# The order of TensorE's work within an attention step: scores, all projection parts, transposes, products, then the tail tasks

## What is computed

```python
q = (x @ Wq).reshape(B, T, H, 2 * DH).transpose(0, 2, 1, 3)      # B=8, T=512, H=16, KV=4, DH=32
k, v = ...                                                        # 4 key/value heads, repeated 4 times
s1 = jnp.einsum('bhtd,bhsd->bhts', q1, k1) * scale + mask         # q1, q2, k1, k2 after rope
s2 = jnp.einsum('bhtd,bhsd->bhts', q2, k2) * scale + mask
diff = softmax(s1) - lam * softmax(s2)
out = jnp.einsum('bhts,bhsd->bhtd', diff, v)
out = group_norm(out, over=(T, 2 * DH)) * gn_w + gn_b
x = layernorm(x + out.reshape(B, T, 2 * H * DH) * (1 - LAMBDA_INIT) @ Wo)
w_e = top-2 weights of softmax(x @ gate_w.T)
x = layernorm(x + sum_e w_e * ((silu(x @ w_gate[e]) * (x @ w_up[e])) @ w_down[e]))
```

## Time and profile before

| | |
|---|---|
| median of 3 runs | 2086.36 us (2084.78 to 2091.78) |
| the profiled execution | 2085.87 us, its span 2084.0 us |
| busy over the span | PE 1708.1 (82%), DVE 1374.3 (66%), ACT 1170.9 (56%), POOL 581.3 (28%) |
| instructions | 37142 |

### The profile page before, as it was taken

The page is one execution under the profiler, slowest core; times in us unless marked ns, Lnnn a source line. Parts: engine busy times, 40 slices in busy tenths (PEclk is TensorE's granted clock), DMA queues, the critical chain, the costliest instruction groups (busy, mean ns, idle before and its releaser), DMA issues. The chain is left out here.

```text
span 2084.0 us, 37142 instructions
## 1 busy us (share of the span) xinstructions
PE 1708.1 (82%) x9698; PEld 1264.6 (61%) x9699; DVE 1374.3 (66%) x3225; ACT 1170.9 (56%) x3378; POOL 581.3 (28%) x496
## 2 busy tenths in 40 slices
PE   4578899899889989889889989873999999999500
PEld 3455556655655655655655655542999999999400
DVE  2578878878888888887887897734333333333366
ACT  2467778787787886877877787832222222222133
POOL 2132232322332232241242243011633332000265
PEclk7799999999999999999999999985999999999755
DMA  7965464565474574565556455213533342232288
GB/s 249 295 168 165 132 169 136 159 177 141 144 211 123 147 214 125 144 199 155 142 173 190 136 166 146 83 67 140 167 118 122 107 127 81 70 101 87 86 283 275
DMA packets 143494, 318.74 MB, mean 153 GB/s; under 512 B 16720, under 2 KB 19408, under 8 KB 141296
## 3 DMA queue, kind: packets, MB, share of 16 engines
q1 hardware_dynamic: 114576, 243.17, 41.1%
q0 software_dynamic: 13792, 46.54, 6.6%
q10 hardware_dynamic: 14976, 27.27, 3.4%
HBM read 215.21 MB, written 109.05 MB: 156 GB/s over the span
## 5 line engine op out<-in xcount | busy, mean ns | idle before, releaser
L803 ACT ACTIVATE expd<-S,neg_max 128x128 f32<-128x128 f32 (+3 forms) x1024 | 531.2, 537 | 167.0 <-DVE neg_max L958 165.1
L958 DVE TENSOR_REDUCE neg_max<-S 128x2 f32<-128x768 f32 (+3 forms) x384 | 399.1, 1039 | 209.9 <-PE S L647 205.4
L989 DVE SCALAR_TENSOR_TENSOR mixed<-expd,rho 128x384 f32<-128x384 f32 (+3 forms) x512 | 328.6, 662 | 0.1
L643 PE MATMUL S<-kT,qT 128*128 128x256 f32 (+2 forms) x1024 | 283.5, 380 | 40.4 <-DMA qT<-parts_rows 25.0
L658 PE MATMUL PTp<-ident,mixed 128*128 128x128 f32 x1280 | 216.9, 285 | 81.7 <-DVE mixed L989 79.4
L815 ACT ACTIVATE probsT<-PTp 128x512 f32<-128x512 f32 (+2 forms) x384 | 205.2, 534 | 122.8 <-PE PTp L658 117.8
L643 PEld LDWEIGHTS S<-kT,qT 128*128 128x128 f32 x1024 | 164.7, 196 | 139.2 <-issue 95.7
L1369 ACT ACTIVATE xT_hi<-xTp 128x512 fp32r<-128x512 f32 x72 | 43.2, 600 | 358.3 <-DVE yo L1545 352.7
L697 PE MATMUL tail<-wo,ctxT 128*128 128x512 f32 x480 | 229.3, 603 | 16.9 <-ACT ctxT L854 9.3
L535 POOL TENSOR_TENSOR swapped<-swapped,rope_t 128x512 f32<-128x512 f32 x80 | 103.3, 1291 | 493.9 <-DVE swapped L951 493.9
L803 ACT ACTIVATION_READ_ACCUMULATOR expd<-S,neg_max 128x1 f32 x1024 | 218.0, 213 | 0.0
(11 more groups left out here) (224 smaller groups left out, 3641.2 us busy)
## 6 DMA issues: line engine op xcount, KB each, us to landing
qT<-parts_rows SPq DMA_DIRECT2D x256, 256.0 KB, 4.5
parts_rows<-parts SPq DMA_DIRECT2D x160, 256.0 KB, 2.1
wqk<-wqk_split SPq DMA_DIRECT2D x75, 512.0 KB, 6.2
xin<-expert_in_rows SPq DMA_DIRECT2D x72, 256.0 KB, 3.0
expert_out_rows<-yo ACTq DMA_DIRECT2D x72, 256.0 KB, 3.2
kT<-parts_rows SPq DMA_DIRECT2D x64, 256.0 KB, 4.4
x<-in_x SPq DMA_DIRECT2D x8, 1024.0 KB, 7.2
x_rows<-x SPq DMA_DIRECT2D x8, 1024.0 KB, 7.2
```

The source lines that it names most:

```text
L643: nc.tensor.matmul(S[s % 2][:, k * slot:k * slot + w], qT[kv % 2][:, 2 * h + c, i * P:(i + 1) * P], kT[kv][:, c, 0:w], start=(k % per_bank ...
L803: ex = nc.scalar.activation(expd[s % 3][:, k * slot:k * slot + w], S[s % 2][:, k * slot:k * slot + w], ACT.Exp, bias=neg_max[s % 3][:, k:k ...
L958: nc.vector.tensor_reduce(neg_max[s % 3][:, 0:k], v, AX, ALU.max, negate=True).then_inc(max_ready, 1)
L989: ins = nc.vector.scalar_tensor_tensor(out=mixed[sl % 3][:, a * 256:a * 256 + w], in0=e2, scalar=rr[:, i, h:h + 1], in1=e1, op0=ALU.mult, ...
```

## The change

`body` of PE calls the same pieces in another order within the step. Before: scores, transposes, parts of groups already begun, tail tasks, parts of a group that begins here, values. After: scores, parts of groups already begun, parts of a group that begins here, transposes, values, tail tasks. All other engines' programs stay as they are.

```diff
                 for s, kv, u in steps(b, first, last):
                     scores(b, s, u, kv)
+                    for new in (False, True):
+                        for idx, c in parts_of(s, last, new):
+                            project(b, first, idx, c)
                     if lagged(b, s, LAG_T, first):
                         transposes(*lagged(b, s, LAG_T, first))
-                    for idx, c in parts_of(s, last, False):
-                        project(b, first, idx, c)
+                    if (s - LAG_V) % NU in LAST_OF and lagged(b, s, LAG_V, first):
+                        values(*lagged(b, s, LAG_V, first), tile_no(b, s, LAG_V))
                     if not first:
                         for task in TAIL_PE.get(s, []):
                             tail_task(b - 1, 1 - par, task)
-                    for idx, c in parts_of(s, last, True):
-                        project(b, first, idx, c)
-                    if (s - LAG_V) % NU in LAST_OF and lagged(b, s, LAG_V, first):
-                        values(*lagged(b, s, LAG_V, first), tile_no(b, s, LAG_V))
```

## The result

The changed kernel is slower: 2116.6 us (median of 4 runs, 2112.1 to 2117.6) against 2089.1 (4 runs of the kernel before beside them, 2084.8 to 2094.6), a ratio of 1.0126 with an interval of 1.0095 to 1.0157. The forecast was 2075 with 2106 as the upper end. The profiled execution took 2115.69 us.

What follows compares the result with a forecast made beforehand. TensorE leads (busy 146.28 of 163.08 us a batch), but VectorE and ScalarE are near full and set the pace in turn. Terms -9.1 +0.7 -1.8 -2.5 +3.9 -2.4 = -11.2 take 2085.9 to 2075; 8-in-10 range 2060 to 2106.

Steps and rivals of the forecast that it cites:

- Steps 45 to 5: Parts fill TensorE's waits for `mixed`; VectorE's max of step 5 starts 1.3 us earlier, carried on: -9.1 us in all.
- Rival 1: The gain is swallowed: VectorE or SP's DMA chain holds step 12 or the stretch behind it; 2084 us, chance 0.20.
- Step 12: ScalarE is the bound to step 17; two parts ahead of the transposes make its copy 0.1 late: +0.7 us in all.
- Steps 16 to 18: Products wait for `ctxT` about 1.1 us; a part fills step 18's wait; step 19 starts 0.25 earlier: -1.8 us in all.
- Steps 24 to 26: Four parts ahead of the transposes; the projection VectorE waits for ends 0.35 earlier, late exps have slack: -2.5 us in all.
- Steps 29 and 31: TensorE waits about 0.45 for `xl` in step 29, products meet `ctxT` 0.2 early in step 31: +3.9 us in all.
- Steps 34 to 43: ScalarE 1.2 late, TensorE waits 2.5 before step 37; early products give back in step 39: net -2.4 us in all.
- rival 3: TensorE's clock falls at step 37 in each of six batches: +12, which gives 2087 us, chance 0.08.
- rule about transposes: PE-mode transposes don't count as busy work for the clock, so those ahead of step 37's wait don't help hold it.
- Rival 2: ScalarE becomes the bound: late transpose copies hold up exps in steps 4, 16, 24 and 34; +23, 2109 us, chance 0.26.
- the signals: Profile signs expected, among them per batch TensorE's `mixed` wait 7.5 to some 5, ScalarE's transpose wait 12.5 to some 20.
- two signs of being wrong: VectorE's reciprocal waits over 0.5 us for exps of steps 4 or 24, or new half-speed stretches appear near step 37.

Runs made afterwards that it cites:

- e4: The changed kernel with GpSimd's low part of group 0 cut to 64 of 512 columns: 2111.9 us, ratio 1.0117.
- e12: e11 with the changed order, parts ahead of the transposes, in steps 2, 4 and 45 alone: 2080.9 us, ratio 0.9958.
- e9: e4 with the weight reload of group 3 cut to 128 instead of 512 KB: 2100.6 us, ratio 1.0058.
- e11: The kernel before with products ahead of the tail in steps 37 to 41, two filling matmuls in step 14, three in step 7: 2074.0 us, ratio 0.9932.
- e6: The changed kernel with transposes ahead of the parts again in steps 12 and 34 alone: 2088.5 us, ratio 1.0003.
- e5: The changed kernel with two filling matmuls ahead of the output projection of step 14: 2098.9 us, ratio 1.0048.
- e1: The kernel before with only the projection parts moved ahead of the transposes, products still last: 2109.5 us, ratio 1.0108.
- e2: The kernel before with only the products moved ahead of the tail tasks, transposes still first: 2083.2 us, ratio 0.9987.

## Why the prediction was wrong, point by point

- **Steps 45 to 5, -1.3: right up to its end, wrong behind it.** The gain was 1.55 + 0.41. The failed step is "Steps 7 to 11 keep DVE as the bound ... the 1.3 us is carried on". I replayed DVE with durations of the timeline as constants. That of `rho` depends on what POOL does at that moment (e4, e12), and step 12 is held by a DMA that does not start earlier just because DVE does (e4, e9, e11). A second step failed just before it: "The exps of step 4 ... start when they did". They start 0.94 later behind their scores, and with them the parts of group 0 and their stores. Rival 1 named this place; its price, nothing left of 9.1, was too mild, as step 12 came 0.85 later than before.
- **Step 12, +0.1: wrong, +1.4 in steps 12 to 16.** The step that failed is the missing term for the clock. Measured from the start of step 12 the norm ends only 0.2 later, not far from the 0.1 of the forecast. But behind a wait that is now 1.76 in every batch the output projection ran at half clock in all of them. Of the 1.47, e6 takes back 1.13 by its order and e5 1.73 by filling alone, so most of it is the clock.
- **Steps 16 to 18, -0.25: the mechanism right, the size off.** PE waits for `ctxT` in step 17, 0.72 in batch 4 (forecast 1.1), and step 18 is shorter by 0.74, but steps 16 to 19 end +0.20. e1 has -0.71 there, e2 +0.11.
- **Steps 24 to 26, -0.35: right.** Steps 23 to 27 gained 0.48 after and 0.47 in e1, and DVE's longest wait for a projection is 1.3 instead of 1.7. What I had not costed is +0.8 in steps 19 to 23, in e1 too. Part of it is a row in each order: two score matmuls of 128x384 that start directly behind the output projection take 0.91 us, behind other matmuls 0.52 to 0.60.
- **Steps 29 and 31, +0.65: too small, +1.13.** The waits for `xl` (0.29 in batch 4) and `ctxT` are there. The rest is again scores behind the output projection, 0.3 each in steps 28, 30 and 32 (e2 shows it alone), of which the products moved away give back about half.
- **Steps 34 to 43, -0.4: wrong, +1.03.** Late exps (+1.2 at step 36) and the early products (-1.66 at step 39) were as forecast; where the clock held, the stretch took what it took before, 31.95: net nothing, not -0.4. The rest is the fall of the clock behind a wait of 2.04, 1.1 to 1.6 us in five of six batches. This is rival 3, priced at 2 us and given 0.08. On the rule about transposes that the prediction names no run here says anything: they stood ahead of this wait in every kernel.
- **Rival 2** was right that late transposes make the kernel slower through ACT, and wrong on where. Steps 16 and 24 have the cover that I named; step 4 hasn't, and step 12 was priced at 0.1. DVE's reciprocal did wait 0.62 for exps, in step 13.
- **The range.** The rivals were priced as if only one could happen. All three did: the gain swallowed, ACT late at two places, and the clock fallen behind both. Six times the errors, 2.4 (5 to 12), 1.4 (12 to 16) and 1.4 (34 to 43), are 31 of the 37 us between -1.6 and +4.6 a batch.

Of the signals, DVE's missing gap before the max of step 5, the waits for `ctxT` and `xl`, no wait before xT(2) and the wait before step 37 (2.04 for 2.5) came. ACT's wait for PTp was 30.6, not 20, and PE's for `mixed` 3.3, not 5. One of the two signs of being wrong came as well: new half-speed stretches at step 37.

**What stays open.** Why, behind the same wait of 1.68 to 1.76 in step 14, the clock fell in all seven batches of the changed kernel, in four of seven in e6 and in two of four before, is not settled. Filling the wait prevents it (e5), but whether the wait of 0.64 in the same step or the one for qT in step 12 tips it was not tried. Nor is it shown how the rest of e9's gain over e4 arises: 1.6 a batch makes 10 of the 11 us, but one profile each is compared.

## What to carry to other kernels

An order that lets the leading engine wait less is worth only what the next lock behind it lets through: follow the gain to the next DMA-held instruction before you count it, and take no duration of VectorE as fixed while GpSimd's instructions move against it. Work put ahead of a producer (here the transposes) is safe where the consumer has slack and costly where the consumer is the bound or has fixed extra work ahead (table loads); order such pieces per step, not by one rule for all: taking back two of 48 steps recovered the whole loss, and five steps carry the whole gain of the best version. When a wait on TensorE grows, price the half-speed stretch behind it as part of the wait.

## What the runs showed of the hardware that was not expected

- An operation of VectorE on one column with its inputs in SBUF took 1.24 us instead of 0.21 when GpSimd's 128x512 low part had started 0.3 us before it; with a low part of 64 columns it took 0.28. In the whole kernel `rho` took over 1 us 24 times before and 42 times after, of 384. An order that moved this operation 1.6 us against the low part made it happen in every batch (e12).
- Behind a wait of 2.04 us in step 37 TensorE's clock fell to half speed in 35 of 42 batches, behind one of 1.21 to 1.35 in 9 of 42. In step 14 it fell in 38 of 51 behind a wait of 1.68 to 1.76. So in step 37 the odds went with the length of the wait, and no single batch could be told by it. A fall cost 0.5 to 2 us.
- From the issue of the stores (256 KB) to that of the first reads behind them it took 6.0 us beside a reload of 512 KB and 4.4 beside one of 128 KB, enough to move the start of step 12 by 1.1 us.
